# Reordered loads and copies in the prologue, and another split of the sums in the last tile, in a kernel of attention and product-key experts

## The reference

```
x = x + attn(layernorm(x))      # 16 query heads of width 8, one key and value head, causal
x = x + ffn(layernorm(x))

# ffn, per token
xn = rmsnorm(x) * gamma
q  = xn @ wq.T                             # 2 halves, 8 heads, 64 wide
sim = einsum('pbnhd,hkpd->pbnhk', q, keys) # 32 keys in each half
sx, ix = top_k(sim[0], 16); sy, iy = top_k(sim[1], 16)
scores, pk = top_k(sx[..., :, None] + sy[..., None, :], 16)   # 16 of 256 pairs
h = gelu(einsum('bnd,bnhkd->bnhk', xn, table_down[indices])) * softmax(scores)
out = einsum('bnhk,bnhkd->bnd', h, table_up[indices])
```

## Time and profile before

| what | value |
|---|---|
| median of three runs | 849.4 us |
| the profiled execution: device time, span | 852.14 us, 850.3 us |
| mean granted TensorE clock | 0.968 |
| VectorE busy | 750.8 us, 88% of the span |
| TensorE busy | 703.9 us, 83% |
| ScalarE busy | 676.8 us, 80% |
| GpSimd busy | 658.2 us, 77% |
| DMA | 32.53 MB, 38 GB/s on average |
| chain that ended last | TensorE 47%, VectorE 25%, issue 14%, ScalarE 9%, DMA 2% |

### The profile page before, as it was taken

The page is one execution under the profiler, slowest core; times in us unless marked ns, Lnnn a source line. Parts: engine busy times, 40 slices in busy tenths (PEclk is TensorE's granted clock), DMA queues, the critical chain, the costliest instruction groups (busy, mean ns, idle before and its releaser), DMA issues.

```text
span 850.3 us, 21025 instructions
## 1 busy us (share of the span) xinstructions
PE 703.9 (83%) x6148; PEld 492.1 (58%) x6214; DVE 750.8 (88%) x2934; ACT 676.8 (80%) x927; POOL 658.2 (77%) x370
## 2 busy tenths in 40 slices
PE   3886878897979888897979888897979888887867
PEld 2652536574646656574646666574646666564746
DVE  4419599999999999999999999999999999898984
ACT  1365688989888898989888898888888898868471
POOL 2111488897979799898979799898979798887761
PEclk9897989999999999999999999999999999899988
DMA  6322121120303121120302021120302121000000
GB/s 176 57 40 56 21 55 28 29 57 10 74 2 67 19 60 26 31 55 10 74 2 67 19 60 26 35 51 10 76 0 67 19 55 27 13 21 1 20 6 7
DMA packets 34736, 32.53 MB, mean 38 GB/s; under 512 B 5520, under 2 KB 32784, under 8 KB 32976
## 3 DMA queue, kind: packets, MB, share of 16 engines
q1 hardware_dynamic: 34608, 32.12, 17.3%
q10 hardware_dynamic: 96, 0.02, 0.0%
HBM read 19.93 MB, written 5.24 MB: 30 GB/s over the span
## 4 chain that ended last, share of the span: by engine, by line
PE 47%; DVE 25%; issue 14%; ACT 9%; DMA 2%; POOL 1%; SPq 1%; DVEq 1%; ACTq 0%; POOLq 0%
DVE prob L1061 12%; PE misc L1305 6%; PE misc L1465 6%; PE score L1342 5%; PE score L1394 5%; PE score L1285 5%; PE score L1255 4%; ACT prob L750 3%; PE score L1287 3%; PE misc L1307 3%; ACT late_scores L616 2%; PE score L1258 2%; DVE halves L901 2%; DVE late_scores L907 2%; PE score L1406 2%
## 5 line engine op out<-in xcount | busy, mean ns | idle before, releaser
L516 POOL TENSOR_TENSOR acc<-acc,prob 128x1024 f32<-128x1024 f32 x184 | 435.5, 2367 | 16.2 <-POOL acc L516 0.6
L1061 DVE SCALAR_TENSOR_TENSOR prob<-score,cut,prob 128x1024 f32<-128x1024 f32 x256 | 314.5, 1277 | 22.8 <-ACT prob L750 21.4
L750 ACT ACTIVATE prob<-score,neg_lse 128x1024 f32<-128x1024 f32 x256 | 279.0, 1119 | 36.8 <-PE score L1394 30.0
L1394 PE MATMUL score<-sel_unit,pieces_t 128*128 128x512 bf16 x479 | 148.2, 395 | 72.5 <-DVE prob L1061 47.5
L643 ACT ACTIVATE probs<-score 128x512 f32<-128x512 f32 x192 | 110.2, 597 | 27.4 <-PE score L1287 23.3
L516 POOL TENSOR_TENSOR acc<-prob 128x1024 f32<-128x1024 f32 x32 | 75.6, 2361 | 64.5 <-DVE prob L1061 64.5
L1394 PEld LDWEIGHTS score<-sel_unit,pieces_t 128*128 128x128 f16 x512 | 40.1, 101 | 118.6 <-DVE prob L1061 83.4
L1342 PEld LDWEIGHTS score<-xn_kept,wdt 128*128 128x128 f32 x480 | 72.4, 191 | 29.4 <-issue 6.4
L1342 PE MATMUL score<-xn_kept,wdt 128*128 128x128 f32 x480 | 85.0, 278 | 3.8 <-DVE prob L1061 3.4
L1255 PE MATMUL score<-k_ahead,q_ahead 128*128 128x256 bf16 (+1 forms) x512 | 70.3, 246 | 12.6 <-ACT probs L643 7.0
L1465 PEld LDWEIGHTS misc<-wu,gated_t 128*128 128x128 f32 x480 | 66.0, 199 | 9.8 <-issue 1.7
(11 more groups left out here) (151 smaller groups left out, 1437.6 us busy)
## 6 DMA issues: line engine op xcount, KB each, us to landing
q_scratch<-qk_piece SPq DMA_DIRECT2D x16, 192.0 KB, 2.1
q_ahead<-q_scratch SPq DMA_DIRECT2D x16, 192.0 KB
q_stack<-q_scratch SPq DMA_DIRECT2D x16, 192.0 KB
xin<-x SPq DMA_DIRECT2D x16, 128.0 KB, 3.0
q_ahead<-q_scratch SPq DMA_DIRECT2D x16, 128.0 KB
q_stack<-q_scratch SPq DMA_DIRECT2D x16, 128.0 KB
xres<-x SPq DMA_DIRECT2D x16, 128.0 KB, 3.4
x_kept<-x SPq DMA_DIRECT2D x16, 128.0 KB, 2.0
```

The costliest lines, as they stand in the source:

```text
L516: eng.tensor_tensor(acc[:, j, :], so_far, prob[:, j * FH + h, :], ALU.add).then_inc(acc_added, FH - h if last else 1)
L750: eng.activation(prob[:, g, :], score[g % BUFS][:, :], ACT.Exp, bias=neg_lse[:, j, h:h + 1]).then_inc(prob_made, 1)
L1061: eng.scalar_tensor_tensor(prob[:, g, :], score[g % BUFS][:, :], cut[:, j, h:h + 1], prob[:, g, :], ALU.is_ge, ALU.mult).then_inc(prob_mas ...
L1394: ins = eng.matmul(score[g % BUFS][:, cols], pieces_t[:, j, h, :], sel_unit[:, cols], start=True, stop=True)
```

## The change

In the prologue the two tables are issued after `stack_pieces(0)` and raise a semaphore of their own, `tables_in`. `fold_keys` waits for the four loads that are left, and VectorE's scaling of `wdt` for the two tables. ScalarE copies `xn_t` before the middle piece of batch 2. TensorE waits for the six score copies of batch 1 and makes five filler matmuls before the transposes of xn, and five after them.

In iteration 0 alone, `scores_for_max(i + 2, 0)` goes behind `weigh_values` on TensorE, and its copy behind `invert_sums` on ScalarE. In iteration 15 alone, ScalarE copies the pieces before `best_exp`.

In the last tile TensorE adds head 2 only, after all score blocks. VectorE adds heads 7, 6, 5, 4 and 3 in a chain of four adds, and TensorE takes that sum up in `finish_last`.

```diff
--- before.py
+++ after.py
@@ -183,6 +183,7 @@
 
 
         weights_in = signal("weights_in")
+        tables_in = signal("tables_in")
         wa_in = signal("wa_in")
         stack_cleared = signal("stack_cleared")
         ident_in = signal("ident_in")
@@ -265,7 +266,7 @@
         prob_made = signal("prob_made", TILES * FH)
         prob_masked = signal("prob_masked", TILES * FH)
         acc_added = signal("acc_added", TILES * (FH - 1))
-        late_added = signal("late_added", 2)
+        late_added = signal("late_added", 4)
         last_hidden = signal("last_hidden", 2)
         last_act = signal("last_act", 2)
         last_gated = signal("last_gated", 2)
@@ -406,8 +407,7 @@
                 eng.dma_start(consts_f, consts).then_inc(consts_in, 16)
                 load_x(1)
                 for dst, src in ((wp[:, :], w_proj), (gam[:, :], gamma), (wqs[:, :], wq.rearrange("k l d -> k (l d)")),
-                                 (keyt[:, :], keys), (wdt[:, :], down),
-                                 (wu[:, :, :], up.rearrange("(c p) d -> p c d", p=P))):
+                                 (keyt[:, :], keys)):
                     eng.dma_start(dst, src).then_inc(weights_in, 16)
                 eng.wait_ge(setup_dve, 3)
                 eng.wait_ge(stack_cleared, 4)
@@ -416,6 +416,8 @@
                 look_ahead(0)
                 load_x(2)
                 stack_pieces(0)
+                eng.dma_start(wdt[:, :], down).then_inc(tables_in, 16)
+                eng.dma_start(wu[:, :, :], up.rearrange("(c p) d -> p c d", p=P)).then_inc(tables_in, 16)
                 load_residual(0)
                 place_max_row(0)
                 store_pieces(1)
@@ -777,8 +779,8 @@
                     max_scores_back(1, w)
                 qk_high_piece(2)
                 v_back(2)
+                xn_back(0)
                 qk_middle_piece(2)
-                xn_back(0)
                 sim_back(0, 0)
                 sim_back(0, 1)
                 sim_high_piece(0, 0)
@@ -802,16 +804,21 @@
                 if f and not a:
                     activate_last(0)
                     activate_last(1)
-                if m:
+                if m and d:
                     max_scores_back(i + 2, 0)
                 if a:
                     invert_sums(i + 1)
+                if m and not d:
+                    max_scores_back(i + 2, 0)
                 if m:
                     max_scores_back(i + 2, 1)
                     max_scores_back(i + 2, 2)
                     max_scores_back(i + 2, 3)
                 if a:
                     x2_back(i + 1)
+                if f and not a:
+                    pieces_back(i, 0)
+                    pieces_back(i, 1)
                 if f:
                     best_exp(i)
                 if m:
@@ -819,6 +826,7 @@
                     max_scores_back(i + 2, 5)
                 if f:
                     log_sum(i)
+                if f and a:
                     pieces_back(i, 0)
                     pieces_back(i, 1)
                 if f:
@@ -1064,11 +1072,11 @@
             def add_late_heads():
 
                 eng.wait_ge(prob_masked, at(prob_masked, LAST, TILES * FH))
-                eng.tensor_tensor(prob[:, 2 * FH - 2, :], prob[:, 2 * FH - 2, :], prob[:, 2 * FH - 1, :],
-                                  ALU.add).then_inc(late_added, 1)
-                eng.wait_ge(late_added, 1)
-                eng.tensor_tensor(prob[:, 2 * FH - 3, :], prob[:, 2 * FH - 3, :], prob[:, 2 * FH - 2, :],
-                                  ALU.add).then_inc(late_added, 1)
+                for n in range(4):
+                    g = 2 * FH - 2 - n
+                    if n > 0:
+                        eng.wait_ge(late_added, n)
+                    eng.tensor_tensor(prob[:, g, :], prob[:, g, :], prob[:, g + 1, :], ALU.add).then_inc(late_added, 1)
 
             def gate_last(j):
 
@@ -1117,7 +1125,7 @@
 
                 eng.wait_ge(wkey_read, 1)
                 eng.tensor_tensor(wkey_sq[:, :], wkey[:, :], wkey[:, :], ALU.mult).then_inc(unit_step, 1)
-                eng.wait_ge(weights_in, 6 * 16)
+                eng.wait_ge(tables_in, 2 * 16)
                 eng.tensor_scalar(wdt[:, :], wdt[:, :], gam[:, 0:1], None, ALU.mult).then_inc(setup_done, 1)
                 eng.wait_ge(norms_made, 1)
                 eng.tensor_reduce(unit[:, :], score[0][:, 0:BANK], AX.X, ALU.max).then_inc(unit_step, 1)
@@ -1206,7 +1214,7 @@
         def _(eng):
             def fold_keys():
 
-                eng.wait_ge(weights_in, 6 * 16)
+                eng.wait_ge(weights_in, 4 * 16)
                 eng.wait_ge(max_kept, every(max_kept, 0))
                 for l in range(LISTS):
                     ins = eng.matmul(score[0][:, BANK + l * KEYS:BANK + (l + 1) * KEYS], wqs[:, l * D:(l + 1) * D],
@@ -1443,8 +1451,8 @@
                 ins.then_inc(acc_tp, 1)
                 eng.wait_ge(acc_added, every(acc_added, LAST))
                 sum_transposed(misc, acc[:, 1, :], False, False)
-                eng.wait_ge(late_added, 2)
-                sum_transposed(misc, prob[:, 2 * FH - 3, :], False, True, acc_tp)
+                eng.wait_ge(late_added, 4)
+                sum_transposed(misc, prob[:, 2 * FH - 5, :], False, True, acc_tp)
                 eng.wait_ge(x2_copied, every(x2_copied, LAST))
                 for j in range(TILES):
                     out_of = score[2][:, j * D:(j + 1) * D]
@@ -1505,7 +1513,10 @@
                 scores_for_max(1, 5)
                 eng.wait_ge(y_t_made, every(y_t_made, 0))
                 project_qkv(2, x2_made, 0)
+                eng.wait_ge(max_kept, every(max_kept, 1))
+                keep_busy(score[1], 5)
                 xn_transpose(0, v_next_made, every(v_next_made, 2))
+                keep_busy(score[1], 5)
                 eng.wait_ge(qk_high, every(qk_high, 2))
                 key_scores(0, 0, qk_rest_made, 2)
                 key_scores(0, 1, xn_t_made, 0)
@@ -1529,11 +1540,13 @@
                     hidden_units(i - 1, 0, range(CH), xn_kept)
                 if f and not a:
                     last_hidden_units(0)
-                if m:
+                if m and d:
                     scores_for_max(i + 2, 0)
                 if a:
                     weigh_values(i + 1, 0, max_t_made, i + 1)
                     weigh_values(i + 1, 1, max_t_made, i + 1)
+                if m and not d:
+                    scores_for_max(i + 2, 0)
                 if m:
                     scores_for_max(i + 2, 1, d)
                     scores_for_max(i + 2, 2)
@@ -1617,11 +1630,10 @@
                 if f:
                     for h in range(4, FH):
                         pair_scores(i, 1, h, a, m)
-                        if not a and h < 7:
-                            sum_last_tile(h - 2)
                         if m:
                             keep_busy(misc[0], 4)
                 if f and not a:
+                    sum_last_tile(2)
                     finish_last()
 
             schedule(eng, prologue, iteration)
```

## The result

The changed kernel takes 847.37 us (median of 9 runs, 845.34 to 849.33); the kernel before, in the same session, 852.01 (9 runs, 849.34 to 855.78). The ratio is 0.9949 with a 95% interval of 0.9928 to 0.9971: 4.3 us faster, between 2.5 and 6.1. The forecast was 7.4. It started from 849.4, the median of three runs; nine runs of the same kernel now give 852.0. So of the 5.4 us between the forecast time of 842.0 and the measured 847.4, 2.6 lie in the starting value. The profiled execution took 848.22 us (span 846.4) against 852.14 (span 850.3), so the two traces show 3.9 us, and these can be placed step by step. Of the changed kernel the first view is that of stretches, with some of 2 us.

What follows compares the result with a forecast made beforehand. VectorE bounds the middle (96% busy, 124 to 806 us), so only prologue, iteration 0 and last iteration can gain. 2.4 + 0.45 + 0.6 + 3.95 = 7.4 us, from 849.4 to 842.0, range 839.2 to 846.0.

Steps and rivals of the forecast that it cites:

- part 3: Iteration 0: TensorE weighs the values before the next maxima scores, so the copy of x2 comes earlier; 0.6 us.
- part 4: Last iteration: ScalarE copies the pieces before the exponentials, so the first exponential of pairs comes earlier; 0.65 us.
- Part 1: Prologue: with the table loads issued later, the first store lands sooner and the first maxima scores start earlier; 2.4 us.
- (d): Rival, prologue: batch 0's max row waits behind the tables in SyncE's queue; total 849.7 us, slower; chance 0.04.
- (a): Rival, prologue: no gain, wq and keys and not the tables slow the first store; total 845.5 us; chance 0.12.
- (b): Rival, last tile: the masks don't close up, since buffers hold the score blocks; total 845.9 us; chance 0.05.
- part 5: Last tile: without sums between score blocks the masks close up, and four chained adds take back some; 3.3 us.
- Part 2: End of prologue: earlier xn copy and TensorE fillers give full-clock key scores and an earlier max row copy; 0.45 us.
- (c): Rival, last tile: with the sums gone, TensorE runs at 1.2 GHz for the whole end; total 848.5 us; chance 0.07.

## Why the prediction was too high

Direction and places were right; the gain was 3.5 us smaller in the traces, 3.9 for 7.4. Three terms account for it (0.97, 1.47 and 1.35 us). Of the others part 3 gave 0.55 more than forecast, and the stretch with part 4 in it 0.25 less.

**Part 1, 2.4 forecast, 1.43 found.** That the tables slowed the store was right, and so the rival in which wq and keys alone keep it slow fell. The step that failed is the upper bound, "2.60, where the filler ends at 22.89 and TensorE is next to be late". I had looked only at the releaser that rows 2 name. The scores need k_ahead as well, issued by ScalarE in 4.55 us after the store; before, it was hidden behind q_ahead, and now it came last. Moving these loads to a queue that is itself on the path gave nothing, which agrees with the Trainium skill, "DMA: Bandwidth & Descriptors", section "Issuing engines are not separate DMA queues": a second issuing engine saves only sequencer time. Here it took 2.26 us of SyncE's. Placed in SyncE's idle time and with fewer fillers, the wait is for q_ahead, and the scores start 7.98 us after the store, where it was 8.33 to 9.01 otherwise: 0.35 to 1.03 us of the forecast were there to be had. The filler's end is no fixed bound either: the same 30 instructions took 4.56 to 6.08 us in the profiles of this case. The gain itself depends on the profile: from the store to the scores the kernel before has 10.39 and 9.74 us.

The tables: 5.7 and 7.0 us to land, from 24.51 and 24.91, as forecast, and the max row did not wait for them: it went out at 36.43. The slower rival, (d), fell. Three sums of the rivals are off, and nothing else rests on them. By the numbers of (d) the row would be 9.5 us late (24.4 + 20.7 - 35.6) and not 7.7. The total of (a), 845.5, leaves out parts 2 and 3 with the store; without part 1 alone it is 844.4. That of (b), 845.9, leaves out part 4 with part 5; without part 5 alone it is 845.3.

**Part 2, 0.45 forecast, -1.02 found.** The key scores reached full clock, 1.95 to 1.96 us in all eleven profiles with the fillers; without them they took 3.42, 2.61 and, in one profile, 1.95. What failed is the sentence that ScalarE's copy "can't come before about 70.67, whatever TensorE does", for it took the fold as fixed. Key scores that end earlier also release the low pieces on GpSimd earlier, right onto VectorE's three last fold steps: 3.14 us for 1.48. Undone, and kept with GpSimd held back, the steps take 1.48 both times; that is shown. I had used this very collision for part 5 and cited the 2.06 us of rows 6, but asked only what the edit does to the engine that it names, not what the faster engine triggers. The rule in "SBUF — State Buffer", "SBUF: two separate sides" (the Trainium skill), by which the operation that starts first keeps the other out for its whole instruction, agrees with both pairs: 1.48 and 3.14, and 1.23 and 2.06 for the wide step. Each GpSimd operation that meets the fold costs 0.83 us: once in the wide step, twice in 3.14, once in the 2.31 of the second profile of the kernel before.

What part 2 costs against the kernel before depends on the profile. From the first of the four score copies to the copy of the max row the kernel before has 11.16 and 11.50 us, the changed one 12.33 to 12.45 in the seven profiles in which the end of its prologue is as it was, and it is 10.78 in the two in which GpSimd stays off the three last fold steps. So part 2 costs 0.8 to 1.3 us against the kernel before, and 1.55 by its undoing (11.41 - 9.86). With GpSimd held back it gains 0.38 over my first profile, close to the 0.45 forecast: the sum was right but for the one wait. Luck has a small share: in that first profile slow key scores happened to keep GpSimd off the fold, which was worth 0.34.

**Part 3, 0.6 forecast, 1.15 found.** The mechanism held, the size was too small. The exchange itself is worth 0.90: from the end of ScalarE's last attention exponential to the copy of x2 it is 9.50 to 9.51 us in all twelve profiles with it, and 10.40 and 10.41 in the two without. The copy of y_t comes 1.81 earlier (1.75 forecast), and the copies between it and x2 take 0.91 more (1.02 forecast). The other 0.25 lie in the attention scores ahead of it, 11.35 us for 11.60. TensorE's clock was 0.99 in 78 to 80 us there, where it had been 0.67. That part was 10.89 to 11.67 in the profiles of the changed versions, so it is no gain of the edit that these runs show. As forecast, VectorE carried the shift through: 1.56 us at x2, 1.32 at neg_lse in the last batch (807.51 for 808.83).

**Part 4, 0.65 forecast, 0.64 found**: the first exponential is 1.96 us earlier, 1.32 of it from before. It starts 0.27 us after neg_lse does and not 0.91. The table has only 0.40 for its stretch because the middle gave back 0.24. That stretch was 713.24 to 716.21 in the profiles of the changed versions, so its length as a whole says nothing about part 4.

**Part 5, 3.3 forecast, 1.95 found** (4.97 - 3.02). The masks closed up as worked out, eight in 9.71 us; rival (b) fell. The first late add did not wait for GpSimd's last (828.91 to 831.28), as I had let it, but started at 830.46 beside it, and the four adds took 5.67 us, 0.63 more than four times 1.26. From the end of the masks to the end of the adds it is 5.70, forecast 5.93 (831.70 to 837.63): that term was right to 0.2. The step that failed is "the last sum starts at 837.68 and ends at 839.63", at 1.95 us. TensorE has nothing to do for 2.76 us while the four adds run, and the sum then takes 3.48 at a clock of 0.50 in 836 to 838. That is rival (c) in another place: I had looked for the slow clock in the stretch before the adds, not in the wait that four adds in a chain make. Both remedies, fillers in the wait and a shorter wait, bring the sum to 2.05. The rule of "TensorE: Matmul & The Clock Gate", "Part 1: The HAM clock gate" (the Trainium skill), that how busy the array has been recently sets the rate, agrees.

Against a tail with the old sums at full clock, part 5 even loses 1.0 us (31.89 for 30.92). In both profiles of the kernel before the first of these sums was slow (3.34 and 3.35 us), in the one profile without part 5 it was not (2.05), and the ratio without part 5 (0.993) against those with it (0.9949, 0.9935), all with intervals that overlap, shows no gain from part 5 that can be measured. So the 1.95 us found are the difference of two profiles, and how much of them is the edit's stays open, as does whether the slow sum belongs to the kernel before or is a draw.

## What to carry to other kernels

When a wait goes, list every semaphore that the waiting instruction needs and when each came; the profile names only the last, and the second to last is the cap of the gain. When an engine is made faster, look at what it releases on the other engines, and whether VectorE is folding beside GpSimd at that moment. When work is moved from TensorE into a chain on VectorE, the idle time that TensorE gets just before the last link of the path is part of the price, and half of the work left on it may be worth more than all of it moved. And before a stretch of two profiles is compared, look how much it differs between profiles of the same kernel.

## What the runs showed that I had not expected

**A tenth of a microsecond on VectorE decides up to 0.7 at the first store.** In the prologue GpSimd's second multiplication for xhat starts at 7.77 us in each profile. Where VectorE's cast of the constants started at 7.79 to 8.63 it took 0.61 us (and a cast that began at 7.79 to 7.83 itself took 1.30 to 1.34, not 0.89); where the cast came at 7.59 to 7.75 it took 1.18 to 1.34, and the first store left at 15.65 to 15.82 in place of 15.1. Here from the run with half of k_ahead before the store:

```profile
7.75 0.89 DVE L1117 CAST cb<-prob 128x1408 bf16<-128x1408 f32 x1 [1.51 <-DMA prob<-consts]
7.77 1.34 POOL L472 TENSOR_TENSOR xhat<-xhat,rstd 128x256 f32<-128x256 f32 x1
```

The second profile of the kernel before (7.71, 1.31 us, store at 15.78) has it too, so it belongs to neither kernel. It is the reason to count the start from the store when two profiles are compared.

**The slow clock after a short wait is regular at one place, and not at another.** In six profiles TensorE waited 2.73 to 2.78 us for the adds, and the last sum took 3.39 to 3.53 each time. After 2.08 us or less it took 2.05, in five profiles. But ahead of the transposes of the run without part 5 TensorE waited 2.62 us, and the clock stayed at 1.00. And in the prologue, where it waits for the q_ahead of batch 1, the clock was down to 0.50 to 0.53 after waits of 1.73, 1.77 and 1.87 us in three profiles, and at 1.00 after waits of 1.54 and 1.83 in two others. Those three have the longest way from the first maxima scores to the score copies, 36.03 to 36.13 us where the others have 34.06 to 35.05; one of the three is the kernel before.
